# A graph network kernel: node chunks run six rounds behind edge blocks in stage two, and 49 stores change stages

## The reference

```
h  = relu(layernorm(x))
# layer 0: messages go from dst to src
gate = silu(edge_attr @ W1.T + b1) @ W2.T + b2 + type_logit(src, dst)
msg  = gate * h[dst] * cutoff(edge_weight) * node_vec[dst]
agg  = segment_sum(msg, src) / clip(segment_sum(node_vec[dst], src), 1e-8)
x    = x + layernorm(h + agg) * gamma + beta
h  = relu(layernorm(x))
# layer 1: messages go from src to dst
h2   = relu(h @ weight1[r] + bias1) @ weight2[r]       # r = 0..7
agg1 = segment_sum(h2[src, edge_type] * edge_weight1, dst)
x    = x + relu(agg1 + bias2)
```

## Time and profile before

| | |
|---|---|
| median of 3 runs | 1534.19 us (1533.41 to 1537.22) |
| profiled execution: own time, span | 1533.91 us, 1532.2 us |
| busy: PE, DVE, POOL, ACT | 1157.1 (76%), 1336.7 (87%), 1025.5 (67%), 618.2 us (40%) |
| DMA | 268.72 MB, mean 175 GB/s |
| mean granted TensorE clock | 0.598 |

### The profile page before, as it was taken

One profiled execution on the slowest core, in us unless ns is written; L12 is line 12 of the kernel. 1 busy time (PEld: TensorE's weight loads), 2 busy tenths in 40 slices (PEclk: granted clock), 3 DMA queues, 4 the chain that ended last, 5 costly groups with the idle time before them and its releaser, 6 DMA issues.

```text
span 1532.2 us, 20105 instructions
## 1 busy us (share of the span) xinstructions
PE 1157.1 (76%) x5198; PEld 846.7 (55%) x5198; DVE 1336.7 (87%) x3937; ACT 618.2 (40%) x1423; POOL 1025.5 (67%) x809
## 2 busy tenths in 40 slices
PE   5898999989999989991047878888888888886000
PEld 2677777777777777771035555555555555554000
DVE  6999999999999999880299999999999999993598
ACT  2544444544445444440034444444444444442000
POOL 7655567777887676666537887887878878866100
PEclk9756555655556565555556565555655655557555
DMA  7999986666666566642446665555555555533899
GB/s 228 305 320 333 325 228 155 153 145 145 142 164 154 136 155 138 147 103 11 130 156 169 170 161 139 140 139 140 138 137 139 140 141 139 140 71 58 295 396 390
DMA packets 154389, 268.72 MB, mean 175 GB/s; under 512 B 73818, under 2 KB 90411, under 8 KB 153380
## 3 DMA queue, kind: packets, MB, share of 16 engines
q1 hardware_dynamic: 78228, 223.53, 43.5%
q0 software_dynamic: 68992, 24.64, 17.5%
q10 hardware_dynamic: 7056, 19.27, 3.1%
HBM read 194.33 MB, written 112.55 MB: 200 GB/s over the span
## 4 chain that ended last, share of the span: by engine, by line
PE 32%; DMA 20%; DVE 19%; POOL 15%; issue 11%; ACT 3%; SPq 1%; POOLq 0%; ACTq 0%; DVEq 0%
POOL agg L468 11%; PE ps_m L555 11%; DMA t<-agg,src_all 6%; PE ps_m L644 6%; PE ps_qs L555 4%; DMA agg<-x,once 3%; PE ps_k L630 3%; DMA lows<-low 2%; DVE x L1038 2%; DVE same L834 2%; DMA agg<-y,once 2%; DVE t L1042 2%; POOL nodes L426 2%; DMA agg<-ysq,once 2%; POOL agg L504 2%
## 5 line engine op out<-in xcount | busy, mean ns | idle before, releaser
L504 POOL DMA_INDIRECT agg<-sums,once x196 | 317.8, 1621 | 89.5 <-issue 64.1
L426 POOL DMA_INDIRECT nodes<-in_table,dst_all x196 | 194.1, 990 | 104.0 <-issue 50.2
L495 POOL DMA_INDIRECT t<-agg,src_all x196 | 190.3, 971 | 83.7 <-issue 49.1
L555 PEld LDWEIGHTS ps_m<-msg,same 128*128 128x128 f32 x980 | 200.4, 314 | 29.8 <-issue 29.8
L555 PE MATMUL ps_m<-msg,same 128*128 128x48 f32 x980 | 208.2, 398 | 1.0 <-issue 1.0
L630 PE MATMUL ps_k<-h_t,rw_sb 56*128 56x256 f32 x588 | 132.3, 571 | 96.3 <-ACT hid L724 73.7
L555 PEld LDWEIGHTS ps_qs<-msg,same 128*128 128x128 f32 x980 | 183.0, 288 | 2.1 <-DVE msg L926 2.1
L555 PE MATMUL ps_qs<-msg,same 128*128 128x49 f32 x980 | 180.1, 362 | 2.0 <-DVE msg L926 2.0
L468 POOL DMA_INDIRECT agg<-x,once x84 | 135.1, 1609 | 49.0 <-issue 21.9
L630 PEld LDWEIGHTS ps_k<-h_t,rw_sb 56*128 56x128 f32 x588 | 67.6, 260 | 144.6 <-ACT hid L724 100.6
L644 PE MATMUL ps_m<-hid,rw_sb 128*64 128x256 f32 x588 | 136.1, 634 | 0.0
(11 more groups left out here) (149 smaller groups left out, 2575.1 us busy)
## 6 DMA issues: line engine op xcount, KB each, us to landing
agg<-in_both SPq DMA_DIRECT2D x14, 2758.0 KB
t<-agg SPq DMA_DIRECT2D x49, 784.0 KB, 4.4
kept<-kept_out SPq DMA_DIRECT2D x49, 404.0 KB, 2.8
kept_in<-kept SPq DMA_DIRECT2D x49, 404.0 KB
agg<-bias_rows SPq DMA_DIRECT2D x49, 384.0 KB
out<-t ACTq DMA_DIRECT2D x49, 384.0 KB, 5.8
rows<-in_src_rows SPq DMA_DIRECT2D x49, 256.0 KB, 4.1
rows<-in_dst_rows SPq DMA_DIRECT2D x49, 256.0 KB, 3.2
```

The lines of the kernel that those rows point to most:

```text
L426: pool.indirect_dma_start(nodes[s][:, t, :], None, table, bass.IndirectOffsetOnAxis(ap=dst_all[:, c:c + 1], axis=0)).then_inc(nodes_in[b % ...
L495: pool.indirect_dma_start(t2[b % T2S][:, t, :], None, wide, bass.IndirectOffsetOnAxis(ap=src_all[:, c:c + 1], axis=0)).then_inc(ends_in[b ...
L504: pool.indirect_dma_start(agg1, bass.IndirectOffsetOnAxis(ap=once1[b % LAG1][:, t:t + 1], axis=0), sums1[b % LAG1][:, t, :], None, compute ...
L555: last = mm(ps[:, t * width:(t + 1) * width], kept_same[:, at:at + P], m[:, v, :], start=(v == t), stop=(v == TILES - 1))
```

## The change

`SKEW` = 6. A round i now pairs edge rows of block i with node rows of chunk i - 6. There are `ROUNDS` = 55 rounds: 0 to 5 have edge rows alone, 6 to 48 both, 49 to 54 node rows alone. `rows_of` gives the rows, and the instructions on v, y, yssq and so on are cut to them. The 49 stores that set `agg1` leave stage one; SP issues them at the beginning of stage two, after two row loads and before the first three chunk loads. `load_chunk` is split into `load_wide` and `load_kept`. POOL's program is unchanged.

```
+SKEW = 6
+ROUNDS = NBLOCK + SKEW
+        def rows_of(i):
+            return slice(0 if i < NBLOCK else TILES, G if i >= SKEW else TILES)
+        def chunk_uses(i):
+            return len(range(i, SKEW - 1, -T2S))
@@ SP, stage one @@
-                while rows_set * (NBLOCK - FILLS) < (b + 1 - FILLS) * NBLOCK:
-                    sp.dma_start(agg1_chunks[rows_set], bias_rows[:, :, :].rearrange("p r w -> p (r w)")).then_inc(S["agg1_set"], 16)
-                    rows_set += 1
@@ SP, stage two @@
+            def load_wide(i):
+                s = i % T2S
+                if i - T2S >= SKEW:
+                    sp.wait_ge(S["x2_done"], i - T2S + 1)
+                sp.dma_start(t2[s][:, TILES:G, :].rearrange("p r w -> p (r w)"), wide_chunks[i - SKEW]).then_inc(chunk_in[s], 16)
+            def load_kept(i):
+                s = i % T2S
+                sp.wait_ge(S["x2_done"], i - T2S + 1)
+                sp.dma_start(kept_in[s][:, TILES * H:TILES * H + KEPT], kept[i - SKEW]).then_inc(kept_got[s], 16)
-            for b in range(T2S):
-                load_chunk(b)
             load_rows1(0)
             load_rows1(1)
             for b in range(NBLOCK):
+                sp.dma_start(agg1_chunks[b], bias_rows[:, :, :].rearrange("p r w -> p (r w)")).then_inc(S["agg1_set"], 16)
+            for i in range(SKEW, SKEW + T2S):
+                load_wide(i)
+            for i in range(ROUNDS):
+                if 2 <= i < NBLOCK:
+                    load_rows1(i)
+                sp.wait_ge(S["x2_done"], i + 1)
+                c, j = i - SKEW, i + T2S
+                if 0 <= c < NBLOCK - RES:
+                    sp.dma_start(x_mid[c], x2[c % 2][:, TILES:G, :].rearrange("p r w -> p (r w)")).then_inc(x_stored[c % 2], 16)
+                if SKEW <= j < ROUNDS:
+                    load_kept(j)
+                    if j >= SKEW + T2S:
+                        load_wide(j)
@@ ACT and DVE, stage two, as examples @@
-            for b in range(-1, NBLOCK + 2):
+            for b in range(-1, ROUNDS):
+                edges, dense = 0 <= b < NBLOCK, SKEW <= b
+                r = rows_of(b)
-                    A(ysq[:, :, :], y[:, :, :], ACT.Square).then_inc(S["ysq_done"], 1)
+                    A(ysq[:, r, :], y[:, r, :], ACT.Square).then_inc(S["ysq_done"], 1)
-                    dve.wait_ge(chunk_in[b % T2S], 16 * uses(b, T2S))
+                    if dense:
+                        dve.wait_ge(chunk_in[b % T2S], 16 * chunk_uses(b))
-                    V.tensor_tensor(v, y[:, :, :], cols(yrstd, H), ALU.mult).then_inc(S["ynrm_done"], 1)
+                    V.tensor_tensor(v[:, r, :], y[:, r, :], cols(yrstd[:, r], H), ALU.mult).then_inc(S["ynrm_done"], 1)
...
```

More of the change, by code:

```diff
@@ L57 @@
 T2S = 3
+SKEW = 6
+ROUNDS = NBLOCK + SKEW
+assert SKEW % 2 == 0 and SKEW > T2S
 FILLS = 14
@@ L698, in _ @@
             sums0_copy(NBLOCK - 1)
-            for b in range(-1, NBLOCK + 3):
+            for b in range(-1, ROUNDS):
                 a, e, f = b + 1, b - 1, b - 2
                 g = b - 3
+                r = rows_of(b)
                 if 0 <= f < NBLOCK:
@@ L707, in _ @@
                     nc.scalar.copy(h2_t[:, :], ps_t[:, 0:BE // 2]).then_inc(S["h2t_copied"], 1)
-                if 0 <= g:
+                if 0 <= g < NBLOCK:
                     act.wait_ge(S["m1t_done"], g + 1)
@@ L733, in _ @@
                     A(hid1[:, 2, :, :], ps_k[0][:, :, 0:BE // 2], ACT.Relu).then_inc(S["relu2_done"], 1)
-                if 0 <= b < NBLOCK:
+                if 0 <= b:
                     act.wait_ge(S["y_done"], b + 1)
                     need(act, S["yssq_done"], b)
-                    A(ysq[:, :, :], y[:, :, :], ACT.Square).then_inc(S["ysq_done"], 1)
+                    A(ysq[:, r, :], y[:, r, :], ACT.Square).then_inc(S["ysq_done"], 1)
                 if a < NBLOCK:
                     act.wait_ge(S["avar_done"], a + 1)
-                    need(act, kept_got[a % T2S], 16 * uses(a, T2S))
+                    need(act, kept_got[a % T2S], 16 * chunk_uses(a))
                     var_at = TILES * H + PC + G
@@ L747, in _ @@
                     A(estd[:, :], evar[:, :], ACT.Sqrt, bias=eps[:, :], scale=1.0 / H).then_inc(S["estd_done"], 1)
-                if 0 <= b < NBLOCK:
+                if 0 <= b:
                     act.wait_ge(S["yvar_done"], b + 1)
                     need(act, S["yrstd_done"], b)
-                    A(ystd[:, :], yvar[:, :], ACT.Sqrt, bias=eps_sq[:, :], scale=1.0 / H).then_inc(S["ystd_done"], 1)
+                    A(ystd[:, r], yvar[:, r], ACT.Sqrt, bias=eps_sq[:, :], scale=1.0 / H).then_inc(S["ystd_done"], 1)
                 if 0 <= f < NBLOCK:
                     act.wait_ge(S["m1_done"], f + 1)
-                if 0 <= g:
+                if 0 <= g < NBLOCK:
                     act.wait_ge(S["sums1_done"], g + 1)
@@ L930, in _ @@
             ST, ES = S2 + PC, S2 + PC + G
-            for b in range(-1, NBLOCK + 2):
+            for b in range(-1, ROUNDS):
                 a, e, d = b + 1, b - 1, b - 2
-                yes = 0 <= b < NBLOCK
+                yes = 0 <= b
+                edges, dense = 0 <= b < NBLOCK, SKEW <= b
+                r = rows_of(b)
+                n = r.stop - r.start
+                c = b - SKEW
+                dest = x_rows(c) if dense else x2[b % 2]
                 on = t2[b % T2S]
@@ L945, in _ @@
                     dve.wait_ge(S["tot_done"], b + 1)
-                    V.reciprocal(rtot[:, :], tot[:, :]).then_inc(S["rtot_done"], 1)
+                    V.reciprocal(rtot[:, r], tot[:, r]).then_inc(S["rtot_done"], 1)
                 if 0 <= e < NBLOCK:
@@ L951, in _ @@
                     dve.wait_ge(S["rtot_done"], b + 1)
-                    dve.wait_ge(kept_got[b % T2S], 16 * uses(b, T2S))
-                    dve.wait_ge(S["astd_done"], b + 1)
-                    V.tensor_tensor(ktot, rtot[:, :], kin[:, ST:ST + G], ALU.mult).then_inc(S["ktot_done"], 1)
+                    if dense:
+                        dve.wait_ge(kept_got[b % T2S], 16 * chunk_uses(b))
+                    if edges:
+                        dve.wait_ge(S["astd_done"], b + 1)
+                    V.tensor_tensor(ktot[:, r], rtot[:, r], kin[:, ST:ST + G][:, r], ALU.mult).then_inc(S["ktot_done"], 1)
                 if a < NBLOCK:
@@ L962, in _ @@
                     need(dve, S["x2_done"], b)
-                    V.tensor_tensor(v, on[:, :, AW:AW + H], cols(ktot, H), ALU.mult).then_inc(S["u_done"], 1)
+                    V.tensor_tensor(v[:, r, :], on[:, r, AW:AW + H], cols(ktot[:, r], H), ALU.mult).then_inc(S["u_done"], 1)
                 if 0 <= e < NBLOCK:
@@ L973, in _ @@
                     dve.wait_ge(S["u_done"], b + 1)
-                    dve.wait_ge(S["apc_done"], b + 1)
+                    if edges:
+                        dve.wait_ge(S["apc_done"], b + 1)
                     need(dve, S["ysq_done"], b)
-                    V.tensor_tensor(y[:, :, :], v, kin[:, 0:S2 + PC].rearrange("p (r f) -> p r f", f=H), ALU.add).then_inc(S["y_done"], 1)
-                if 0 <= d:
+                    V.tensor_tensor(y[:, r, :], v[:, r, :], kin[:, 0:S2 + PC].rearrange("p (r f) -> p r f", f=H)[:, r, :], ALU.add).then_inc(S["y_done"], 1)
+                if 0 <= d < NBLOCK:
                     dve.wait_ge(rows_in[d % 2], 16 * (uses(NBLOCK - 1 - d % 2, 2) + uses(d, 2)))
@@ L982, in _ @@
                     dve.wait_ge(S["asq_done"], a + 1)
-                    dve.wait_ge(kept_got[a % T2S], 16 * uses(a, T2S))
+                    need(dve, kept_got[a % T2S], 16 * chunk_uses(a))
                     V.tensor_reduce(kin_a[:, ES:ES + TILES], asq[:, :, :], AX_X, ALU.add).then_inc(S["avar_done"], 1)
@@ L992, in _ @@
                     dve.wait_ge(S["ysq_done"], b + 1)
-                    V.tensor_reduce(yssq[:, :], ysq[:, :, :], AX_X, ALU.add).then_inc(S["yssq_done"], 1)
-                if 0 <= d:
+                    V.tensor_reduce(yssq[:, r], ysq[:, r, :], AX_X, ALU.add).then_inc(S["yssq_done"], 1)
+                if 0 <= d < NBLOCK:
                     dve.wait_ge(S["same1_done"], d + 1)
@@ L999, in _ @@
                     dve.wait_ge(S["yssq_done"], b + 1)
-                    dve.wait_ge(S["avar_done"], b + 1)
+                    if edges:
+                        dve.wait_ge(S["avar_done"], b + 1)
                     need(dve, S["ystd_done"], b)
-                    V.scalar_tensor_tensor(out=yvar[:, :], in0=kin[:, ES:ES + G], scalar=EPS, in1=yssq[:, :], op0=ALU.mult,
+                    V.scalar_tensor_tensor(out=yvar[:, r], in0=kin[:, ES:ES + G][:, r], scalar=EPS, in1=yssq[:, r], op0=ALU.mult,
                                            op1=ALU.add).then_inc(S["yvar_done"], 1)
@@ L1020, in _ @@
                     dve.wait_ge(S["ystd_done"], b + 1)
-                    V.reciprocal(yrstd, ystd[:, :]).then_inc(S["yrstd_done"], 1)
+                    V.reciprocal(yrstd[:, r], ystd[:, r]).then_inc(S["yrstd_done"], 1)
                     dve.wait_ge(S["yrstd_done"], b + 1)
```

(13 more changed lines are left out.)

3 lines of the change are left out of this document (1 added, 2 removed).

## The result

The changed kernel takes 1541.56 us (median of 19 runs, 1535.51 to 1547.04) against 1534.19 (19 runs, 1525.5 to 1541.39): ratio 1.0044, 95% interval 1.003 to 1.0057. It is slower by 7.4 us; 1539 was forecast, with 1524 to 1552 as its range. The profiled execution has a span of 1541.5 us, 9.3 more than before.

The account below looks back on a forecast made before the run. POOL's scatter-adds bound the ends of both stages, POOL's loop the full rounds, transfers the final stage. Terms -10 - 5 + 16.5 + 3.7 = +5.2 gave a path ending at 1537.4, forecast as 1539 us; range 1524 to 1552.

Parts of the forecast that it names:

- The stores leave stage one: Stage one: without 49 stores, 27% of its queue's bytes, the scatter-adds end 10 us sooner; bounds nothing to 40 us.
- T: End of the last scatter-add of stage one (add0): 743.5 us before, forecast 733.5.
- the 740: Sign: stage two's first gather near 733 us; above 740 refutes the stage-one saving.
- a disturbance of 40 us: Stage one: POOL's 529.3 us of scatter-adds against 489 at undisturbed prices; other traffic costs 40 us.
- The first agg1 add at T + 55: Start of stage two: POOL's first add waits for the moved stores, yet starts 5 us sooner than T + 59.9.
- The full rounds keep POOL's pace: Rounds 5 to 48 of stage two: POOL's loop keeps 12.97 us a round; change 0.
- Six chunk rounds: Rounds 49 to 54, 8.7 us each: 54.4 us with edge remainders, 16.5 beyond POOL's drain of 37.85.
- The cold beginning of the final stage: Four x_mid loads, formerly done during POOL's drain, now precede the first agg load: 3.7 us more, bounds 0 and 5.
- Rival A: Stage one: the stores were the disturbance; more than 15.2 us saved, kernel faster, 1524 at 25 us; chance 0.20.
- C: Start of stage two: stores at 325 GB/s, first agg1 add at T + 65, 10 us later, 1549; chance 0.11.
- D: Final chunk rounds: 11.8 us each from bare handovers between VectorE and ScalarE, 19 us more, 1558; chance 0.11.
- B: Stage one saves 14 to 18 us, tail as priced, so it cancels: 1533; chance 0.13.

Follow-up runs that it names:

- The double dose: SKEW = 4 with stores in stage one, each store issued again into an unused tensor; 1546.63 us, ratio 1.0042 to the kernel before.

## Why the prediction was right

Its steps, in its own order:

1. The stores leave stage one: -10 forecast, T came 5.5 us earlier in the pair of profiles, 0.6 of it because the first add0 did; 5.8 is the difference of the means over all. The first gather at 738.39 is close to the 740 that I had named as refuting this step. It is the mis-sized term. I gave the stores their share of bytes (27%) of a disturbance of 40 us; what went is 14% of it.

   The waits for landings, which I had in mind, did shrink as I said, by 13.2 us in the pair (68.7 to 55.5) and by 9 in the mean. But in the pair 4.8 us came back as waits of POOL for ScalarE and VectorE (3.0 to 7.8, the longest 3.91), and 3.5 in POOL's own instructions and the gaps between them. So "the saving isn't cut by another engine" didn't hold in this pair; in the means over all profiles these engines' waits differ by less than 1 us, and what they took here may be scatter.

   I had also written that the prediction is wrong if the disturbance isn't linear in bytes. The double dose indicates, in its one profile, that it isn't: by my own sign the reasoning of this step fails, though the total stands. Which of the other transfers and waits make up the rest of the 40 us wasn't tried. A slip beside it: 49 stores of 384 KB are 19.27 MB, not 18.87, a share of 28%, which moves the term by less than 1 us.
2. The first agg1 add at T + 55: 56.2 in both profiles of the changed kernel, ended by the stores; the sums of block 0 forecast at T + 46 stood at T + 44 (ScalarE's copy at 781.96 lies 44.0 after T). The stop at the mask of block 2 came, until T + 65.1 rather than T + 62, and cost at most the 1.16 us of the second add group; full stays at 583 us. The margin to T + 66 was thinner than I made it.
3. The full rounds keep POOL's pace: 583.5 forecast, 583.3 measured.
4. Six chunk rounds: 54.4 forecast, 52.4 measured (8.27 us for a bare round rather than 8.7), so 14.5 us stick out beyond what the drain used to cover, against 16.5. SKEW of 4, 6 and 8 show it step by step: the final stage begins at 46.4, 60.3 and 77.3.
5. The cold beginning of the final stage: 3.7 forecast, 8.00 - 3.24 = 4.8 measured. The final stage took 0.5 us less.

Sum measured: -5.5 - 3.7 - 0.2 + 14.5 + 4.8 - 0.5 = +9.4, the difference of the spans (9.3) but for rounding; forecast +5.2. Rival A is refuted: the stores weren't the disturbance. C, slow stores, and D, chunk rounds of 11.8 us, didn't occur. B wanted 14 to 18 us from stage one and got 5.5. Step 1 is off by 4.5 us, nearly as much as the whole sum; the errors of the other steps (+1.3, -0.2, -2.0, +1.1, -0.5) cancel, and that is luck. What the runs bear out is the mechanism of steps 2 to 4; that the median came within 3 us of 1539 says little of step 1.

## What to carry to other kernels

Work taken from a covered place and put after the last covered round costs its full bare price; before it is paired anew, count how many rounds the drain behind it can hold: here four, not six. Transfers that are moved to the head of a queue delay everything that shares it, and the first to feel it is the earliest reader, which may be one pipeline step ahead of the round that the load is named after. Two halves of a change should be run apart: here one was neutral, the other a loss, neither told what the two together would cost, and the part that helped (fewer rounds of skew, stores left where they were) was in neither.

## What the runs showed of the hardware

A queue of 49 stores of 384 KB held the issuing engine for 51.91 us, 1.06 us each, although single issues take 0.32 us to 0.43 us (the load of `agg` in SP's queue above). The first two took 0.90 us together, the median of all is 1.04, and a store landed 4.1 to 6.5 us after its issue, 5.0 in the median. I read it as a queue that takes only so many in advance, after which the issuer moves at the pace of the transfers; 5.0 / 1.06 gives an estimate of five stores under way. The limit itself wasn't tried. This core's stores and gathers together ran at 389 GB/s. The Trainium skill (DMA: Bandwidth & Descriptors, Specifications) gives about 358 GB/s of memory bandwidth for one core, worked out as half of what two cores share. Here one core ran alone and moved more; the measurement decides. The wait for a scatter-add's landing doubled from 2.3 to between 4.3 and 4.8 us beside the 49 stores in a row; the longest in stage one with two doses was 5.08 us, and single waits of 4.1 us stand in the changed kernel, which has no such stores there. That fits what the Trainium skill says of turns between queues on each DMA engine (DMA: Bandwidth & Descriptors, Queues, rings and completion order); the runs don't isolate it.
